# A mixture-of-experts, state-space, mixture-of-experts block: in its second feed-forward stage, the routing of group 1 moved ahead among single shared pairs

## The reference

```python
x = x + 0.5 * ffn(layernorm(x))
x = x + attn(layernorm(x))          # in_proj, conv, silu, state-space scan, gate, norm, out_proj
x = x + 0.5 * ffn(layernorm(x))     # the same weights as the first

def ffn(x):                         # 16 experts, 4 of them for each token, and a shared one
    tidx, tw = route(x, router_weight, e_bias)        # sigmoid scores, 2 of 4 groups, top 4, weights
    h = silu(x @ gate_w[e].T) * (x @ up_w[e].T)       # for each expert e of the token, inner width 128
    routed = sum over the 4 experts of tw * (h @ down_w[e].T)
    shared = silu(x @ sh_gate.T) * (x @ sh_up.T) @ sh_down.T   # width 256, done as 2 units
    return routed + shared
```

## Time and profile before

| | |
|---|---|
| median of 3 runs | 1458.34 us (1457.24 to 1463.23) |
| the profiled execution, span | 1457.1 us |
| PE busy | 1277.6 us (88%) |
| POOL busy | 971.7 us (67%) |
| DVE busy | 893.7 us (61%) |
| ACT busy | 626.6 us (43%) |
| second feed-forward stage | from about 1003 us (its first tiles are routed under the attention stage) to the end |

### The profile page before, as it was taken

The page is one execution under the profiler, slowest core; times in us unless marked ns, Lnnn a source line. Parts: engine busy times, 40 slices in busy tenths (PEclk is TensorE's granted clock), DMA queues, the critical chain, the costliest instruction groups (busy, mean ns, idle before and its releaser), DMA issues.

```text
span 1457.1 us, 23386 instructions
## 1 busy us (share of the span) xinstructions
PE 1277.6 (88%) x6904; PEld 1101.4 (76%) x6904; DVE 893.7 (61%) x2190; ACT 626.6 (43%) x1088; POOL 971.7 (67%) x1340
## 2 busy tenths in 40 slices
PE   5697999999967699999999999996988399999990
PEld 5595888888855578888888887785877388888870
DVE  5765722354628997877878787767657322354553
ACT  2153344444315456566566565561342134434420
POOL 3588880584848597787978879531757870384876
PEclk9898999999988899999999999997989799999995
DMA  9974585687743201000000000214434464587753
GB/s 353 410 276 170 167 305 180 213 281 234 240 160 134 91 2 44 16 30 16 30 30 29 29 0 30 81 30 167 176 134 168 134 241 167 196 263 251 233 173 113
DMA packets 86919, 218.43 MB, mean 150 GB/s; under 512 B 16272, under 2 KB 28560, under 8 KB 85904
## 3 DMA queue, kind: packets, MB, share of 16 engines
q1 hardware_dynamic: 62224, 149.82, 28.8%
q0 software_dynamic: 24576, 67.14, 14.6%
HBM read 109.43 MB, written 107.48 MB: 149 GB/s over the span
## 4 chain that ended last, share of the span: by engine, by line
PE 50%; DVE 17%; POOL 14%; issue 12%; ACT 3%; DMA 3%; POOLq 0%; DVEq 0%; SPq 0%; ACTq 0%; another core or an unknown queue 0%
PE ps L1082 10%; POOL f_gbuf L493 8%; PE ps L1116 8%; PE ps L1087 6%; PE ps L1050 4%; DVE at_xs L1854 4%; PE ps L2054 4%; PE ps L2056 4%; PE ps L2055 4%; PE ps L2115 3%; POOL xg L467 2%; PE ps L1066 2%; PE ps L2104 1%; PE ps L2116 1%; DMA f_gbuf<-yg,f_rows 1%
## 5 line engine op out<-in xcount | busy, mean ns | idle before, releaser
L493 POOL DMA_INDIRECT f_gbuf<-yg,f_rows x256 | 268.4, 1048 | 214.9 <-DMA yg<-f_yo 155.1
L467 POOL DMA_INDIRECT xg<-f_xn,f_rows x256 | 251.8, 984 | 113.6 <-DVE f_rows L770 59.7
L1082 PE MATMUL ps<-f_wgu,f_xT 128*128 x1248 | 297.4, 381 | 3.1 <-DVE f_hT L823 3.1
L1082 PEld LDWEIGHTS ps<-f_wgu,f_xT 128*128 128x128 f32 x1248 | 226.4, 191 | 28.0 <-issue 3.3
L819 DVE TENSOR_TENSOR f_h<-ps,f_sg 128x256 f32<-128x256 f32 x156 | 66.0, 423 | 248.5 <-ACT f_sg L547 247.7
L1116 PE MATMUL ps<-f_wd,f_hT 128*128 x624 | 163.7, 385 | 39.7 <-ACT f_yo L556 20.7
L547 ACT ACTIVATE f_sg<-ps 128x256 f32<-128x256 f32 x156 | 59.9, 384 | 313.6 <-PE ps L1082 313.6
L843 DVE SCALAR_TENSOR_TENSOR f_xin<-f_gbuf,f_w,f_xin 128x256 f32<-128x256 f32 x256 | 125.4, 490 | 75.4 <-DMA f_gbuf<-yg,f_rows 68.3
L1116 PEld LDWEIGHTS ps<-f_wd,f_hT 128*128 128x128 f32 x624 | 117.9, 192 | 61.0 <-issue 45.4
L1087 PE MATMUL ps<-f_xT,f_wgu_sh 128*128 128x256 f32 x512 | 132.5, 413 | 23.7 <-DVE f_hT L823 23.7
L1854 DVE SCALAR_TENSOR_TENSOR at_xs<-at_raw,at_taps,at_xs 128x512 f32<-128x512 f32 x136 | 140.2, 1033 | 8.1 <-POOL at_xs L1505 3.9
(11 more groups left out here) (258 smaller groups left out, 2708.3 us busy)
## 6 DMA issues: line engine op xcount, KB each, us to landing
f_xq<-xg SPq DMA_DIRECT2D x78, 512.0 KB, 4.1
yg<-f_yo SPq DMA_DIRECT2D x156, 256.0 KB, 2.9
xg<-f_gbuf SPq DMA_DIRECT2D x39, 512.0 KB, 17.8
f_wgu<-in_gate_up SPq DMA_DIRECT2D x4, 1280.0 KB, 15.3
f_xin<-in_x SPq DMA_DIRECT2D x8, 512.0 KB, 7.0
xg<-f_xn,f_rows POOLq DMA_INDIRECT x256
f_gbuf<-yg,f_rows POOLq DMA_INDIRECT x256, 3.8
x<-f_xin SPq DMA_DIRECT2D x8, 512.0 KB, 4.0
```

Source lines behind the costliest of these rows:

```text
L467: G.indirect_dma_start(xg[0:USED[g] * P, :], bass.IndirectOffsetOnAxis(ap=rows[g][:, b, k:k + 1], axis=0), xn[:, SUB * TILE0[g] + b, :], N ...
L493: G.indirect_dma_start(gbuf[:, n % GBUF, k, :], None, yg[0:USED[g] * P, :], bass.IndirectOffsetOnAxis(ap=rows[g][:, b, k:k + 1], axis=0), ...
L1082: last = T.matmul(gu_ps[:, j % 2, s * 2 * P:(s + 1) * 2 * P], x_of(k, s, d), weight(wgu[:, :, d, :], experts[s]), start=(d == 0), stop=(d ...
```

## The change

All of it concerns the second stage (`fresh` false), except that some shared code is written in another way with the same result for the first.

- The events up to the first routed pair become: route 0 to 5; shared 0; route 6, 7; shared 1, 2; route 8, 9; shared 3; route 10, 11; shared 4, 5, 6; route 12, 13; shared 7; route 14, 15; shared 8, 9. There are no "both" events: pairs 6 to 9 are turned twice. Units, downs and routers are as many as before, and the routed pairs and shared 10 to 15 stand where they stood.
- Group 1 is counted behind shared 6 in place of route 15, and its pieces 5 and 6 follow there.
- Statistics, shifts and normalizing of tiles 3 to 7 are tied to other events; POOL calls `rstd_of` for tiles 4 to 7 behind blocks 0, 1, 2 and 3.
- `store_tile` waits for `part_out` too; `combine` waits for a part if it was taken before it, `take_part` for the combine if that was first. `LATE` is 1, which leaves the pieces of group 2 where they were.

```diff
-SECOND_NORMALIZE = {("route", 1): 2, ("shared", 2): 3, ("both", 6): 4, ("both", 8): 5, ("route", 10): 6, ("shared", 4): 7}
+SECOND_NORMALIZE = {("route", 1): 2, ("route", 5): 3, ("route", 7): 4, ("route", 9): 5, ("shared", 5): 6, ("route", 13): 7}
@@ ffn_events, fresh false
+        yield from each("shared", 0)
+        yield from each("route", 6, 7)
+        yield from each("shared", 1, 2)
+        yield from each("route", 8, 9)
+        yield from each("shared", 3)
+        yield from each("route", 10, 11)
+        yield from each("shared", 4, 5, 6)
+        yield from each("route", 12, 13)
+        yield from each("shared", 7)
+        yield from each("route", 14, 15)
+        yield from each("shared", 8, 9)
@@
-    COUNT_AT = [("shared", 0) if fresh else ("route", 5), ("route", 15), ("routed", (0, 5))]
+    LATE = 1
+    COUNT_AT = [("shared", 0) if fresh else ("route", 5), ("route", 15) if fresh else ("shared", 6), ("routed", (0, 4 + LATE))]
@@
         def store_tile(t):
             sp.wait_ge(combined, SUB * (t + 1))
+            sp.wait_ge(part_out, max(part_of(2 * t), part_of(2 * t + 1)))
@@
-                if fresh and g == 0 and b < 4:
+                if g == 0 and b < 4:
                     rstd_of(4 + b)
-                if not fresh and g == 0 and b in (1, 2, 4, 6):
-                    rstd_of({1: 4, 2: 5, 4: 6, 6: 7}[b])
@@ take_part
+            before = [n for n in added if n // 2 == r]
+            if before:
+                dve.wait_ge(combined, before[-1] + 1)
+            parts.append(r)
@@ combine
-            dve.wait_ge(part_out, outputs_before(("both", "shared"), [m for _, m in OUTPUTS].index(r)) + 1)
+            if r in parts:
+                dve.wait_ge(part_out, part_of(r))
+            added.append(n)
@@ second_duties
             if (kind, n) == ("route", 5):
                 route_piece(0, 5)
                 route_piece(0, 6)
+                statistics(4)
             if (kind, n) == ("shared", 0):
+                statistics(5)
+            if (kind, n) == ("route", 6):
+                shift_of(4)
+            if (kind, n) == ("shared", 2):
+                shift_of(5)
+            if (kind, n) == ("route", 8):
                 route_piece(0, 7)
-            if (kind, n) == ("shared", 1):
-                statistics(4)
-            if (kind, n) == ("shared", 2):
-                statistics(5)
+            if (kind, n) == ("route", 9):
+                statistics(6)
+                route_piece(0, 8)
             if (kind, n) == ("shared", 3):
-                shift_of(4)
-                route_piece(0, 8)
-            if (kind, n) == ("both", 6):
                 route_piece(0, 9)
-                statistics(6)
-            if (kind, n) == ("both", 7):
-                shift_of(5)
                 statistics(7)
-            if (kind, n) == ("both", 9):
+            if (kind, n) == ("route", 11):
+                route_piece(1, 0)
+            if (kind, n) == ("shared", 4):
                 shift_of(6)
-            if (kind, n) == ("route", 11):
+                route_piece(1, 1)
+            if (kind, n) == ("shared", 5):
                 shift_of(7)
-                route_piece(1, 0)
-                route_piece(1, 1)
-            if (kind, n) == ("shared", 4):
                 route_piece(1, 2)
-            if (kind, n) == ("route", 15):
+            if (kind, n) == ("shared", 6):
                 route_piece(1, 5)
                 route_piece(1, 6)
-            if (kind, n) == ("shared", 5):
+            if (kind, n) == ("shared", 7):
                 route_piece(1, 7)
```

More of the change, by code:

```diff
@@ L94, in ffn_events, with each @@
 def ffn_events(fresh):
[L96 to L103, removed]
-    if fresh:
-        for r in range(2, 4):
-            yield "shared", r
-    else:
[L108 to L116, removed]
+    def each(kind, *pairs):
+        for r in pairs:
+            yield kind, r
+    yield from each("route", 0, 1, 2, 3, 4, 5)
+    if fresh:
+        yield from each("shared", 0, 1)
+        yield from each("both", 6, 7, 8, 9)
+        yield from each("route", 10, 11)
+        yield from each("shared", 2, 3)
+        yield from each("route", 12, 13, 14, 15)
+        yield from each("shared", 4, 5, 10, 11)
+    else:
+        yield from each("shared", 0)
[3 more added lines that the diff above has]
+        yield from each("shared", 3)
+        yield from each("route", 10, 11)
+        yield from each("shared", 4, 5, 6)
[3 more added lines that the diff above has]
+        yield from each("shared", 8, 9)
     for g in range(NG):
@@ L120, in ffn_events @@
         if g == 0 and not fresh:
[L121 to L124, removed]
+            yield from each("shared", 10, 11)
+    yield from each("shared", 12, 13, 14, 15)
 UNITS_OF = {"route": 0, "both": SH, "shared": SH, "routed": 1}
@@ L183, in combine, with stored_from @@
         return self.of_pair(USED[g] // 2 - 1) + DOWN_ROUTED + COMBINE + 8 * b // 5
+    def stored_from(self, s):
+        return min(n for n in range(sum(RP)) if self.of_pair(n) + DOWN_ROUTED >= s)
     def stored_ahead_of(self, g, b):
@@ L336, in ffn_stage @@
     ROUTES = [(k, n) for k, (kind, n) in enumerate(EVENTS) if kind in ("route", "both")]
-    COUNT_AT = [("shared", 0) if fresh else ("route", 5), ("route", 15), ("routed", (0, 5))]
-    PACK_AT = [("both", 6) if fresh else ("shared", 3), ("shared", 5) if fresh else ("routed", (0, 1)), ("routed", (0, 11))]
+    LATE = 1
+    COUNT_AT = [("shared", 0) if fresh else ("route", 5), ("route", 15) if fresh else ("shared", 6), ("routed", (0, 4 + LATE))]
+    PACK_AT = [("both", 6) if fresh else ("shared", 3), ("shared", 5) if fresh else ("routed", (0, 1)), ("routed", (0, 10 + LATE))]
     shifted = DIRECT if fresh else 0
@@ L352, in outputs_before, with part_of @@
         return sum(kind in kinds for kind, _ in OUTPUTS[0:yy])
+    def part_of(r):
+        return outputs_before(("both", "shared"), [m for _, m in OUTPUTS].index(r)) + 1
     SLOTS = Slots(EVENTS)
@@ L498, in gather_group @@
                         rest()
-                if g == NG - 1 and b in (2, 3, 4):
+                if (g, b) in ((2, 2), (2, 3), (2, 4)):
                     next(other, None)
@@ L827, in take_hT @@
             V.tensor_copy(hT[:, j % 4], hT_bank[SLOTS.routed_before(j) % 2][:, 0:2 * P]).then_inc(hT_copied, 1)
+        added, parts = [], []
         def take_part(s, yy):
@@ L996, in after @@
                 second_duties(kind, n)
-            if kind == "routed" and n[0] == 0 and n[1] > 0:
-                route_piece(2, n[1] - 1)
+            if kind == "routed" and n[0] == 0 and n[1] >= LATE:
+                route_piece(2, n[1] - LATE)
             if (kind, n) in FINAL:
```

## The result

| | before | after |
|---|---|---|
| median of the runs | 1458.38 us (1457.24 to 1463.23, 5 runs) | 1452.99 us (1451.26 to 1454.15, 5 runs) |
| ratio, 95% interval | | 0.9953 (0.9937 to 0.9970) |
| profiled span | 1457.1 us | 1452.1 us |
| POOL idle ahead of group 1, for `f_rows` | 14.43 us | 0.3 us |
| POOL waits for `f_var` in group 0 | 3.82 us | 7.60 + 2.65 us |

By the medians the change makes the kernel 5.4 us faster, where 6.1 were forecast; by the ratio it is 6.9 us (4.4 to 9.2). Both lie inside the half per cent, 7.3 us.

What follows compares the result with a forecast made beforehand. POOL from 1013 to 1158 us was taken as the bound: 14.4 - 0.3 + 3.8 - 11.4 = 6.5 us, taken as 6.1, gave span 1451.0 and, with 1.2 added, 1452.2 us. The range was 1446.5 to 1458.5.

Steps and rivals of the forecast that it cites:

- The bound: Second feed-forward stage: POOL from 1013 to 1158 us, then SP's release, sets PE's pause and the end, one to one.
- the sum: Gain at group 1's start: 14.4 - 0.3 + 3.8 - 11.4 = 6.5 us, taken as 6.1 by start times.
- POOL's 18.2 us of waits: POOL's waits up to group 1: 14.4 us for f_rows plus 3.8 for f_var, all this stage can give.
- Routing off the path: Group 1's rows on DVE: ready near 1074 us instead of 1096, so POOL's 14.4 us wait falls to 0.3.
- The cover: Ahead of group 1: its rows are ready 17 us before POOL wants them.
- The new waits for `f_var`: POOL in group 0: 8.7 us for tile 6 and 2.7 for tile 7, in all 11.4 in place of 3.8.
- the low clock behind PE's idle time: PE's slots from 1016.1 us: 1.2 GHz level behind the gap adds 3.0 us, so the slot ends at 1032.1.
- the in-order argument: DVE runs statistics 6 behind take_part of shared 1, which can't pass PE, making tile 6's f_var 8.7 us late.
- PE's arrival: First routed turn 8.0 us later, PE at the pause by 1152.6 at most; release still decides by 8.8 us on ACT.
- The port: DVE's row instructions under POOL's scatters: contention by the skill's rule, but the trace shows next to none.
- the fourth rival: DVE's 10.4 us of row instructions each stop POOL: 6.1 becomes -4.3, time 1462.6 us; chance 0.05.
- The first rival: Statistics come sooner: 1449.2 us if PE keeps 2.4 GHz, 1444.2 if POOL waits no longer than before; chance 0.23.

Runs made afterwards that it cites:

- e8: e1 with the loads of quads 8, 9 and 10 issued behind store_y(8) instead of store_y(2), (4) and (6) in the second stage: 1432.69 us, ratio 0.9808.
- e5: The changed kernel with group 1 counted, and its pieces 5 and 6 done, behind route 15 again: 1451.55 us, ratio 0.9942.
- e1: The changed kernel with POOL's rstd_of for tiles 6 and 7 moved back behind blocks 4 and 6 of group 0: 1444.39 us, ratio 0.9885.
- e6: The changed kernel with both rstd_of(6), (7) behind blocks 4 and 6 and group 1 counted behind route 15: 1452.75 us, ratio 0.9946.
- e4: The changed kernel with PE turning eight pairs (route 12 to 15, shared 6 to 9) three times instead of once: 1453.96 us, ratio 0.9953.
- e9: The changed kernel with loads of quads 8, 9 and 10 issued behind store_y(8) instead of store_y(2), (4) and (6): 1443.96 us, ratio 0.9882.
- e3: The changed kernel with statistics(4) moved behind the two gates of shared 0, ahead of statistics(5): 1455.65 us, ratio 0.9950.
- e11: The changed kernel with PE turning eight pairs (route 12 to 15, shared 6 to 9) nine times instead of once: 1458.01 us, ratio 0.9981.

## Why the prediction was right, step by step

- **The bound.** POOL from the first scatter to the last of group 1, then SP's release, then PE: confirmed by the one-to-one shift over nine kernels (table). Two things in this part of the prediction are wrong. The 73.6 us are SP's wait for the first quad, that of group 0; for the ninth it waited 33.8 us, as the waits of the kernel before from 1100 to 1170 show (total, times, longest):

```profile
SPq L377 <- DMA xg<-f_xn,f_rows: 33.8, 1, 33.8
```

No term of the sum used the 73.6. And POOL's 18.2 us of waits are not "all that this stage can give": that holds only while quad 8 stands ahead of the stores of y. With the loads later in SP's list, e8 is more than 25 us under the kernel before.
- **Routing off the path.** Rows were forecast 61 us after the first scatter (1074 against 1013.15) and came at 62.3 (1077.7 against 1015.42). My count had missed that PE's turn of shared 4 waits for `f_words`, 3.28 us behind DVE's pieces, and that low clock follows (3.5 us, below). That is more than the 1.4 us by which the rows came later, so other parts of the hand count were too long. The cover was 14.3 us instead of 17. The changed kernel didn't need the early count (e5); in e1 it is worth 8 to 10 us (e6), and the rows are there 3.9 us ahead of POOL.
- **The new waits for `f_var`.** Forecast 8.7 and 2.7, measured 7.60 and 2.65. The first is the mis-sized term: the low clock behind PE's idle time was put at 3.0 us, by the earlier trace rows, and cost 1.9 (a down of 3.58 us start to start in place of 1.73, then all at full clock: granted 0.58 in 1018 to 1022.5, where the stretch behind the gap in the earlier trace rows had 0.52). All of this reached `f_var`, as the in-order argument said.
- **What e5 corrects.** The sum booked 14.1 us as won by the early count and 7.6 us net as lost to the statistics. The total of that booking is right, but the early count as such could have been left where it was: the maximum of two ready times was moved on one side only, and the new order alone had moved it far enough. The prediction named the cover of 17 us but didn't draw from it that a later count would do.
- **PE's arrival.** Forecast: first routed turn 8.0 us later, PE at the pause by 1152.6 at most, ACT freed 8.8 us after it gets there. Measured, less the 2.27 us of the later start: 1094.9, 1151.1, and 9.48 us. The extra turns cost nothing (e4).
- **The port.** During the rows of group 1 (1067 to 1078) ten scatters took 972 to 1078 ns, median 973, and the 48 scatters and four rstds of group 0 take 66.47 us in e1 with DVE's row work under them: 61.3 us for 48 scatters, as in group 1 before, and 4 x 1.25 make 66.3, so next to nothing is left over. By the Trainium skill, page "SBUF — State Buffer", section "Who interferes with whom", a part of these DVE instructions could shut POOL out for their length; no run here shows it, and the fourth rival falls.
- **The end.** From the first scatter the changed kernel is 7.27 us faster; 2.27 us of that were given back in this profile by a later start of the stage, so that span and median moved by 5.0 and 5.4. That term was not in my working. Its like shows in kernels with nothing changed ahead of it (1013.09 in e5, 1017.77 in e9), and the ratio's 6.9 us (4.4 to 9.2) can't tell how much of it there is on average. 1.7 of the 2.27 us are there when the attention stage starts (first `at_tap` at 496.57 before, 498.26 after); what they come from stays open. So it is partly luck that 5.4 lies so near 6.1: the sum was 1.2 us short, nearly all of it the low clock's term, and the later start took more than that back.

The first rival named 1444.2 for statistics that come sooner, with the old 3.8 us of waiting left. e1 measured 1444.39 in another way: POOL asks later, no wait is left, and group 1 starts 17.3 us earlier than before. Its ratio alone would give 1441.6, so the agreement to 0.2 us is chance; what it bears out is that POOL's waits are worth their length.

## What to carry to other kernels

Where a stage's start is the later of two ready times, moving one of them is worth only what the other leaves. Look up both before and after, and count what the move queues onto the second. An in-order queue that both computes something small for others and starts the transfers that all wait for should meet each small task no earlier than its input is ready: here two 1 us instructions, moved 8 and 12 scatters ahead of where they stood, cost 10 us. A load that waits long, standing in a list ahead of stores that are ready, stops the producer of these stores; put it as late as its own consumer allows.

## What the runs showed of the hardware

- The low clock behind an idle time of PE has no fixed price. Before the change, 3.0 us were lost after 5.05 us idle. In the kernels with the new order the same down behind 5.95 to 5.98 us idle took 3.21 to 3.58 us start to start in place of 1.73, a loss of 1.5 to 1.9 us; behind 3.17 us idle in e3, 1.6 us. In the changed kernel 11.71 us idle cost 3.2 us, and 3.28 us idle in front of 1044.07 cost 3.5: the turn, two routers, down, turn and two units behind it took 11.2 us, where full clock would take 7.8, at a granted clock of 0.70.
- In e11, with 28.2 us of added transposes, PE kept its clock at 1.00 from 1085 to 1165, and only 3.5 to 5.0 us of them showed.
- The time from the start of the program to the stage's first scatter differs by 5.4 us among profiles of kernels whose work up to there is all but the same, more than the effect of several edits here. A stage is better measured from its own first event.
